# A selective-scan kernel: two states stacked on the partitions, all scan inputs turned on TensorE

## The reference

```python
xz = einsum('bld,ed->ble', x, W_in); xc, z = split(xz, 2)       # 256 inner channels each
xc = silu(causal_conv4(xc) + conv_b)
dbc = einsum('ble,re->blr', xc, W_x)                            # 8 for dt, 16 for B, 16 for C
dt = softplus(einsum('blr,er->ble', dbc[..., :8], W_dt) + b_dt)
A = -exp(A_log)                                                 # 256 x 16 states
def step(h, inp):                                               # over the 32 tokens
    h = exp(dt_t[:, :, None] * A) * h + (dt_t * x_t)[:, :, None] * B_t[:, None, :]
    return h, einsum('bdn,bn->bd', h, C_t)
y = (ys + xc * D_skip) * silu(z)
out = einsum('ble,de->bld', y, W_out)
```

## Time and profile before

| | us |
|---|---|
| three runs, median (lowest, highest) | 848.93 (847.19, 849.27) |
| span of the profiled execution | 847.5 |
| PE busy | 764.2 (90%) |
| DVE busy | 750.4 (89%) |
| ACT busy | 727.1 (86%) |
| POOL busy | 713.4 (84%) |

### The profile page before, as it was taken

How to read it: one execution, slowest core, us unless ns; L and a number is a source line. 1 busy time by engine, 2 the same in 40 slices (tenths; PEclk the granted TensorE clock), 3 DMA queues, 4 the chain that set the end, 5 groups by cost and what they waited for, 6 DMA issues and landing times.

```text
span 847.5 us, 13089 instructions
## 1 busy us (share of the span) xinstructions
PE 764.2 (90%) x4510; PEld 386.1 (46%) x4510; DVE 750.4 (89%) x476; ACT 727.1 (86%) x1301; POOL 713.4 (84%) x337
## 2 busy tenths in 40 slices
PE   8788989999999999898999998989999987678998
PEld 5534434343435453434353533434444433337876
DVE  2798999999999999999999999999999999984241
ACT  4889999999999999999999999999999999545050
POOL 0658999999999999999999999999999999980000
PEclk9799989999999999999999999999999999799999
DMA  7808071544335251527070717262534436000001
GB/s 201 299 4 272 26 250 52 184 143 158 144 113 189 84 210 57 229 67 260 29 271 28 251 51 251 76 223 79 195 108 145 159 101 224 2 1 1 1 37 63
DMA packets 39146, 110.97 MB, mean 131 GB/s; under 512 B 7244, under 2 KB 9384, under 8 KB 39080
## 3 DMA queue, kind: packets, MB, share of 16 engines
q1 hardware_dynamic: 37724, 109.84, 37.2%
q10 hardware_dynamic: 1356, 0.29, 0.2%
HBM read 106.97 MB, written 3.15 MB: 130 GB/s over the span
## 4 chain that ended last, share of the span: by engine, by line
DVE 27%; POOL 21%; PE 19%; issue 18%; ACT 12%; SPq 2%; DMA 1%; DVEq 0%; POOLq 0%; ACTq 0%
DVE state L894 13%; POOL state L598 10%; DVE bank L894 10%; POOL state L589 10%; PE bank L1283 8%; PE bank L1089 4%; ACT bank L694 3%; PE bank L1082 3%; ACT product L718 3%; ACT state L705 2%; DVE state L904 2%; POOL u L612 1%; ACT L753 1%; ACT dt L758 1%; SPq L406 1%
## 5 line engine op out<-in xcount | busy, mean ns | idle before, releaser
L598 POOL TENSOR_TENSOR state<-state,wide 128x1024 f32<-128x1024 f32 x161 | 378.1, 2368 | 10.0 <-DVE state L894 10.0
L589 POOL TENSOR_TENSOR state<-u,wide 128x1024 f32<-128x1024 f32 x128 | 301.7, 2369 | 11.9 <-PE bank L1089 11.7
L1089 PE MATMUL bank<-state,ident 64*64 64x512 f32 x2048 | 264.1, 627 | 0.5 <-POOL state L598 0.3
L894 DVE TENSOR_TENSOR_SCAN state<-state,bank 128x1024 f32<-128x1024 f32 x95 | 214.9, 2272 | 2.8 <-PE bank L1082 2.8
L718 ACT ACTIVATE product<-u_tok,b_tok 128x256 f32<-128x256 f32 x512 | 213.0, 499 | 2.3 <-PE bank L1082 1.8
L1082 PE MATMUL bank<-ident,product 128*128 128x128 f32 x1024 | 143.4, 285 | 67.9 <-ACT product L718 32.4
L1082 PEld LDWEIGHTS bank<-ident,product 128*128 128x128 f32 x1024 | 115.7, 146 | 164.2 <-issue 95.9
L694 ACT ACTIVATE bank<-dt,a_neg 128x512 f32<-128x512 f32 x256 | 166.0, 680 | 25.5 <-DVE state L894 16.8
L705 ACT ACTIVATE state<-dt,a_neg 128x512 f32<-128x512 f32 x256 | 167.0, 715 | 0.6 <-PE bank L1089 0.6
L894 DVE TENSOR_TENSOR_SCAN state<-bank,state 128x1024 f32<-128x1024 f32 x66 | 149.9, 2270 | 0.8 <-ACT bank L694 0.8
L894 DVE TENSOR_TENSOR_SCAN bank<-bank,state 128x1024 f32<-128x1024 f32 x62 | 141.6, 2284 | 3.8 <-ACT bank L694 2.9
(11 more groups left out here) (101 smaller groups left out, 509.3 us busy)
## 6 DMA issues: line engine op xcount, KB each, us to landing
wide<-bc_rows SPq DMA_DIRECT2D x176, 512.0 KB, 6.2
wide<-bc_rows SPq DMA_DIRECT2D x32, 256.0 KB, 3.5
x_t<-in_x_dram SPq DMA_DIRECT2D x4, 512.0 KB, 4.8
out_dram<-x_t SPq DMA_DIRECT2D x8, 256.0 KB, 2.0
k_room<-in_L_conv_w_dram SPq DMA_DIRECT2D x2, 576.0 KB, 4.7
bc_rows<-dbc SPq DMA_DIRECT2D x16, 64.0 KB, 1.6
state<-in_L_conv_W_in_dram SPq DMA_DIRECT2D x2, 256.0 KB, 3.9
x_tok<-in_x_dram ACTq DMA_DIRECT2D x1, 256.0 KB, 3.7
```

The costliest lines, as they stand in the source:

```text
L589: pool.tensor_tensor(tile(n), u[:, :, :], over_halves(b_wide[:, PLAIN.index(s), :]), ALU.mult).then_inc(plain_input, 1)
L598: pool.tensor_tensor(tile(n), tile(n), over_halves(c_wide[:, n % NST, :]), ALU.mult).then_inc(output_pool, 1)
L894: dve.tensor_tensor_scan(flat(target), flat(decay), flat(source), 0.0, ALU.mult, ALU.add).then_inc(scanned, 1)
L1089: return pe.matmul(y_sum[64 * h:64 * h + 64, b, :], weights[rows, :], source[rows, h, :], start=first, stop=last)
```

## The change

Two states now share a tile's partitions. A tile still has 128x1024, and an item still has 16 of them, but tile `2j + h` holds states `2j` and `2j + 1` (`STACK = 2`) of half of the channels: partition = 64 b + 32 i + c, with `i` the state of the pair. With this

- all inputs are turned: every state's product with B is made in token order, seven states' on ACT and nine states' on POOL (`POOL_B`, `products`), and PE turns all 16 tiles; every decay goes to SBUF and reads dt and A doubled to the stacked layout. dt is doubled by eight DMAs an item from SBUF to SBUF (`duplicate_dt`), A_log by eight loads;
- only C is broadcast, by four DMAs a pair of states to 32 partitions each (`spread_c`); B needs no broadcast;
- the sum over states is done by 64x32 blocks: the two tiles of a pair go to different columns, and each block adds two states (`sum_states`);
- POOL has eleven products with C and DVE five; `SLOTS` is 13 instead of 9; the order tables are new, and PE has 20 slots;
- the output is projected and added in quarters, 256 columns in each item from the fifth on, and all x groups are turned ahead of the first tile; the signs of the 3x3 weights are turned in one go in item 0 (`PE_KERNELS`, `ACT_KERNELS`), straight to the weights of the convolutions;
- ACT leaves out the table load between the gate and the softplus (`EXP_BETWEEN` is false), and the two rows of W_dt stand at different partitions (`DT_AT`).

The core of the diff:

```diff
-SLOTS = 9
+SLOTS = 13
-PRODUCTS = 3
+PRODUCTS = 2
-POOL_C = (0, 1, 2, 3, 7, 8, 10, 12, 14, 15)
+STACK = 2
+POOL_B = (2, 3, 4, 5, 6, 8, 10, 11, 14)
+ACT_B = tuple(e for e in range(NST) if e not in POOL_B)
+POOL_C = (0, 1, 2, 4, 5, 6, 8, 9, 10, 11, 14)
+PE_TAPS = {3: ((1, 4),), 4: ((1, 5), (1, 6), (1, 7)), 11: ((2, 0), (2, 1)), 12: ((2, 2),), 13: ((2, 3),)}
+PE_TURNS = {1: (0,), 2: (1,), 3: (2,), 4: (3,), 5: (4,), 6: (5,), 7: (6,), 8: (7,), 9: (8,), 10: (9,), 11: (10,),
+            12: (11,), 13: (12,), 15: (13,), 16: (14,), 17: (15,)}
+PE_SUMS = {0: (-4,), 1: (-3, -2), 2: (-1,), 8: (0,), 14: (1,), 15: (2,), 16: (3,)}
+POOL_PRODUCTS = {0: (5, 6), 1: (8,), 2: (10, 11), 4: (14,), 5: (18, 19, 20)}
+POOL_OUTPUTS = {0: (0,), 1: (1, 2, 3), 2: (4,), 3: (5, 6, 7, 8), 5: (9, 10, 11, 12, 13, 14, 15)}
+ACT_DECAYS = {0: (4, 5, 6, 7, 8), 3: (9, 10, 11, 12, 13), 5: (14,), 6: (15, 16), 7: (17, 18, 19)}
+ACT_PRODUCTS = {0: (7,), 1: (9,), 3: (12, 13), 4: (15,), 6: (16, 17)}
+ACT_KERNELS = (2, 2, 2)
+PE_KERNELS = 10
...
+            def duplicate_dt(k):
+
+                sp.wait_ge(dt_ready, HALVES * (k + 1))
+                wait(sp, decay_ready, HALVES * NST * (k - 1))
+                for b in range(2):
+                    for i in range(STACK):
+                        for q in range(2):
+                            first, source = 64 * b + CH32 * i, 64 * b + CH32 * q
+                            sp.dma_start(dt_dup[k % 2][first:first + CH32, q:q + 3:2, :],
+                                         dt[source:source + CH32, :, :]).then_inc(dup_loaded, 16)
...
             for k in range(ITEMS):
                 store_rows(k)
+                for j in range(STATE_PAIRS):
+                    if j == SP_DUP:
+                        duplicate_dt(k)
+                    spread_c(k, j)
...
-            def times_b(n):
+            def products(e):
+                wait(pool, u_tok_ready, 4 * k + 4)
+                wait(pool, b_tok_ready, k + 1)
+                wait(pool, turned_input, 2 * (e // STACK - PRODUCTS + 1))
+                for blk in range(BLOCKS):
+                    pool.tensor_scalar(state_product(e)[:, blk, :, :], by_pair(u_tok[:, blk, :]),
+                                       b_tok[k % 2][:, blk, i:i + 1], None, ALU.mult).then_inc(product_pool, 1)
...
+            def decays(n):
...
+                k, j, h = n // NST, n % NST // 2, n % 2
+                wait(act, dt_far, k + 1)
+                wait_slot_free(act, n)
+                for q in range(2):
+                    g = 2 * h + q
+                    act.activation(tile(n)[:, q, :], dt_dup[k % 2][:, g, :], ACT.Exp,
+                                   scale=a_st[k % 2][:, j, g:g + 1]).then_inc(decay_ready, 1)
...
-                    copy(u_tok[:, 2 * j:2 * j + 2, :].rearrange("p a d -> p (a d)"), work[1]).then_inc(u_tok_ready, 1)
+                    for b in range(2):
+                        copy(u_tok[:, 2 * j:2 * j + 2, :].rearrange("p a (g i c) -> p (a g) i c", i=2, c=CH32)[:, :, b, :],
+                             work[1].rearrange("p (g i q c) -> p g i q c", g=4, i=2, q=2)[:, :, b, :, :]).then_inc(u_tok_ready, 1)
...
             def scan(n):
...
+                wait(dve, turned_input, n + 1)
+                wait(dve, decay_ready, HALVES * (n + 1))
                 target = tile(n) if by_pool(n) else pair[n % PAIRS]
-                dve.tensor_tensor_scan(flat(target), flat(decay), flat(source), 0.0,
+                dve.tensor_tensor_scan(flat(target), flat(tile(n)), flat(pair[n % PAIRS]), 0.0,
...
             def turn_input(n):
...
+                i, h = n // 2, n % 2
+                if h == 0:
+                    wait(pe, product_act, products_of(ACT_B, i + 1))
+                    wait(pe, product_pool, products_of(POOL_B, i + 1))
                 wait_pair_free(pe, n)
                 for blk in range(BLOCKS):
-                    for h in range(HALVES):
-                        mm = pe.transpose(pair[n % PAIRS][:, h, 128 * blk:128 * blk + 128],
-                                          product[j % PRODUCTS][:, blk, 128 * h:128 * h + 128], ident[:, :])
+                    for q in range(2):
+                        g = 2 * h + q
+                        mm = pe.transpose(pair[n % PAIRS][:, q, 128 * blk:128 * blk + 128],
+                                          product[i % PRODUCTS][:, blk, 128 * g:128 * g + 128], ident[:, :])
...
-                wait_output(pe, n)
-                for b, h in QUARTERS:
-                    mm = sum_quarter(b, h, ident2[:, :], tile(n), False, n % NST == NST - 1)
+                for n in (2 * i, 2 * i + 1):
+                    wait_output(pe, n)
+                    for b, q in QUARTERS:
+                        g = 2 * (n % 2) + q
+                        rows = slice(64 * b, 64 * b + 64)
+                        mm = pe.matmul(y_sum[CH32 * g:CH32 * g + CH32, b, :], ident4[rows, :], tile(n)[rows, q, :],
+                                       start=False, stop=(j == STATE_PAIRS - 1))
+                    mm.then_inc(summed, 1)
```

More of the change, by code:

```diff
@@ L75 @@
+ACT_PRODUCTS = {0: (7,), 1: (9,), 3: (12, 13), 4: (15,), 6: (16, 17)}
+ACT_EARLY = {}
+PE_SLOTS = 20
+PE_Z = 5
 PE_DBC = 6
 PE_DT = 7
[L77 to L89, removed]
+PE_B_TOK = 10
+PE_U_TOK = (14, 15)
+ACT_XC = 0
+ACT_GATE = 1
+ACT_DBC = 2
+ACT_DT = 2
+ACT_B_TOK = 4
+ACT_U_TOK = (5, 6)
+POOL_U = 3
@@ L91 @@
+POOL_FAR = 4
+SP_DUP = 2
+EXP_BETWEEN = any(s in ACT_DECAYS for s in range(ACT_GATE + 1, ACT_DT + 1))
+LATE_SUMS = sum(e < 0 for pairs in PE_SUMS.values() for e in pairs)
+LATE_OUTPUTS = sum(e < 0 for tiles in POOL_OUTPUTS.values() for e in tiles)
+DVE_POST = 3
+DVE_OUT = 8
 POST_INSIDE = True
-AT_KERNELS = (8, 9, 10)
-LAST_POOL = tuple(s for s in DVE_C if 8 <= s <= 12)
+ACT_SIGNS = 1
+ACT_KERNELS = (2, 2, 2)
+PE_KERNELS = 10
+LAST_POOL = tuple(s for s in DVE_C if 8 <= s <= 11)
 AT_STATS = 8
@@ L360, in flat, with over_quarters, state_product, by_pair @@
             return halves.rearrange("p h n -> p (h n)")
-        def over_halves(row):
-            return row.unsqueeze(1).to_broadcast([128, HALVES, CHUNK])
+        def over_quarters(row):
+            return row.unsqueeze(1).to_broadcast([128, 2, CHUNK])
+        def state_product(e):
+            i, j = e // STACK, e % STACK
+            return product[i % PRODUCTS][:, :, :].rearrange("p a (g i c) -> p a g i c", i=STACK, c=CH32)[:, :, :, j, :]
+        def by_pair(blk_tokens):
+            return blk_tokens.rearrange("p (g c) -> p g c", c=CH32)
+        def products_of(states, pairs):
+            return BLOCKS * before(states, STACK * pairs)
         def res_half(n):
@@ L425, in small_groups @@
                      w_x[m][:, :, :].rearrange("p a e -> p (a e)")),
-                    ("small", m, [w_dt_raw[m][:, h, :] for h in range(HALVES)], 128, (BC, XROWS), w_dt[m][BC:, :])]
+                    ("small", m, [w_dt_raw[m][:, h, :] for h in range(HALVES)], 128, (0, XROWS), w_dt[m][:, :])]
         def out_group(m):
@@ L784, in _ @@
                     for e in ACT_DECAYS.get(s, ()):
-                        if NST * k + e > 0:
-                            plain_decays(NST * k + e)
-                    for e in ACT_TURNED.get(s, ()):
                         if NST * k + e >= 0:
-                            turned_decays(NST * k + e)
+                            decays(NST * k + e)
                     prepare(k + 1, s)
-                    if k == 0 and s < 3:
-                        setup_copy(act, copy, BY_ACT[s - 3], setup_act)
+                    if k == 0:
+                        kernels(s)
                     for e in ACT_PRODUCTS.get(s, ()):
```

472 lines of the change are left out of this document (217 added, 255 removed).

## The result

The changed kernel takes 1096.6 us (median of 4 runs, 1093.8 to 1099.3) against 848.9 us (847.2 to 849.3) in the same session: a ratio of 1.293, with a 95% interval of 1.291 to 1.295. The forecast was 837 us. The profiled span is 1097.4 us.

What follows compares the result with a forecast made beforehand. DVE's chain was taken to set the pace, with POOL full as well. Profiled span 847.5 + 3 (start and first item) - 15 (fourteen items) = 835.5, plus 1.4 to the median: 837 us; likeliest 830 to 846, wide range 825 to 882.

Steps and rivals of the forecast that it cites:

- POOL's t: Time of each of POOL's 36 small products an item, in 27.6 us plus 36 t: 0.36 to 0.38 us, bounds 0.2 and 0.59.
- Rival One: POOL becomes the bound at its 36 small products, deciding from t = 0.43; total 866 us at 0.5, 911 at 0.59; chance 0.22.
- Rival Two: PE's sums over states: the eight blocks don't run beside each other; PE 50.0 us an item, 928 us in all; chance 0.07.
- Rival Three: Passage through two PSUM pairs eats the gain: period stays at 44.6 us, total time 849 to 855 us; chance 0.14.
- Rival Four: The start costs nothing and DVE has no new stall: 829 us or less; chance 0.09.
- one step less: DVE makes five C products instead of six: 1.35 us less an item, period 43.22 us if the stalls stay.
- the 0.3 us of stall that I added: DVE's added wait an item, for turned tiles passing two PSUM pairs, raising the period to 43.5 us.
- ACT: 40.8 against 40.8: ACT's work an item: fewer products, one table load less, narrower copies; 40.8 us, nothing for writing in runs of 32 columns.
- I had 41.9: PE's work an item: 8.9 us more for transposes, 8.2 less for sums over states; 41.9 us.
- The bytes moved: Data moved by the loads and other DMAs: claimed to fall to under half.
- The first scan: Start of the kernel: more loads and the decay's waits put DVE's first scan at 41 us instead of 32.8.
- The first item: Item 0: 43.5 + 5 = 49 us instead of 54.2, with a DVE stall of some 5 us ahead of scan 9.

Runs made afterwards that it cites:

- the fastest version: Against the 853.9 us version: dt's duplication before the C loads, convolution weights' loads behind them, their magnitudes and signs in first items, tiles 12 and 13's decays later; 823.7 us.

## Why the prediction was wrong, step by step

**The failed step** is POOL's t: "I take 0.36 to 0.38, because the new instruction also reads one tensor". It is 0.902 us. 27.6 + 36 x 0.902 = 60.1 us, and the period is 60.54: the equation was right, and the one number in it that no row showed was out by a factor of 2.4. Both ends of its bound failed for a reason that the runs name. Below, I took POOL's selections as relatives because they too read one tensor; their 0.05 us for 64 columns is 0.8 ns a column, the product with a scalar has 2.5. (0.29 + 2 x 0.05 is 0.39 us, not 0.40; it changes nothing.) Above, I took a quarter of the two-tensor product, 0.59 us, as a ceiling. That takes it that a form with one tensor is not dearer per column than one with two, and that a quarter of the columns is a quarter of the time; here the columns of the scalar form cost 2.5 ns, against 1.68 with the column held still and at most 2.3 (2.32 us/1024) in the moving product that I quartered, and an instruction has 0.14 or 0.26 us of its own, by its form. The two-tensor product of 256 columns, at 0.572 us, would just have kept the bound.

The Trainium skill's figure for short bodies of one input (GPSIMD Engine Reference, section Elementwise — side-by-side cycle accounting, 1.03 cycles an element), which gave the estimate of 0.22 us, doesn't hold for this instruction, with its 2.5 ns a column; its 2.6 cycles an element for `tensor_tensor`, an estimate of 2.2 ns a column at 1.2 GHz, agrees with the 2.32 us for the 1024 columns of the product with C, but not with the 1.68 ns of the product whose second operand stands still.

**Rival One** was the mechanism, from its own deciding point (0.43) on; its price ended at 911 us because its t ended at 0.59.

**Rival Two** falls: the sums are 119.8/14 = 8.6 us an item against 16.4 in the earlier trace rows, so eight blocks run side by side as four did: 7.8 us less, where I took 8.2. **Rival Three** falls by the run with three quarters of POOL's C products left out, and by the fastest version, which leaves out nothing and has a period of 42.99 us. **Rival Four** falls: the start did cost.

**What held.** DVE: one step less gave 44.57 - 1.35 = 43.22 us; the run that relieves POOL has 42.96, without the 0.3 us of stall that I added. ACT: 40.8 against 40.8, and its products at 163.8/392 = 0.418 us lose nothing by the broken write. PE: I had 41.9; it is 550.40/14 = 39.3 where the granted clock is 0.99 of full speed, and 617.95/14 = 44.1 after, at 0.88. The bytes moved fell from 110.97 to 60.43 MB, not quite to half.

**What was mis-sized.** The first scan: 46.1 us after, not 41. I named three parts (A_log's issues, the magnitudes behind the weights, dt's duplication). The version that moves all three, and the second item's taps, has it at 36.8; no run splits their sum. A_log's eight issues and the x copy behind them:

```profile
3.98 5.11 ACTq L418 DMA_DIRECT2D gate<-in_L_conv_A_log_dram  x8
...
10.41 0.60 ACT L661 ACTIVATE x_t<-bank 128x512 f32<-128x512 f32 x1
```

The pieces cost 0.64 us each, not 0.25 to 0.49, and the copy came 4.3 us later than in the earlier trace rows. That cost more than the delay. PE stood idle for 4.01 us before its first taps, and ran them from 11.07 to 17.20 us at a mean granted clock of 0.59 of full speed, for the most part at the lower of its two levels (1.2 GHz). Eight records of the same kind took 3.60 us from 19.44 us on at 1.00, the upper level (2.4 GHz), and 3.61 at the start of the kernel before, where PE had no such idle time. These 2.6 us were in no term of mine.

```profile
11.07 6.16 PE L1073 MATMUL bank<-x_t,w_tap 128*128 128x512 f32 x8 [4.01 <-ACT x_t L661]
...
19.44 3.60 PE L1073 MATMUL bank<-x_t,w_tap 128*128 128x512 f32 x8
```

The first item, where POOL's C products are cut to a quarter, takes 53.1 us, not 49 (43.5 + 5 is 48.5): besides the 5.25 us ahead of scan 9, which I had, DVE waits there 5.6 us for turned tiles, which I hadn't. That run's 838.6 us stand close to my 837 by luck, because errors cancel: against my sum +6.0 (first scan at 47.0), +4.1 (first item), -7.6 (period), -1.3 (last item 51.3) and +0.1 behind it.

## What to carry to other kernels

Before work is moved to an engine in a form that its trace doesn't show, let the range reach as far as the form can go: a bound from another instruction held here neither for a smaller size nor for another kind of operand. On GpSimd a column held still as the second tensor, in one instruction over all blocks, did in 1.87 us what four products with a scalar did in 3.6; with that form, one state's product moved to ACT and the orders changed, the stacked kernel runs in 0.972 of the time of before. And where one engine has no rest, a part moved to it is multiplied by its count: 36 x 0.52 us more than I took is 18.8 us, sixteen times.

## What the runs showed of the hardware

- A GpSimd product of a tensor and a scalar per partition (fp32, 128 partitions, 256 and 512 columns): 0.26 us fixed and 2.5 ns a column; 0.09 us less for 256 columns if the scalar is a number. Eight runs of 32 columns cost as much to write as one of 256 (0.902 and 0.898 us).
- A GpSimd product of two tensors whose second operand stands still along the columns: 0.14 us fixed and 1.68 ns a column (0.572 us for 256, 1.865 for 1024). The product with C, with a moving one, took 2.32 us for 1024.
- DVE scanning or idle made no difference to the step of the product with a scalar (0.902 us beside both).
- TensorE: eight blocks of 64x32 run beside each other as four of 64x64 did: 119.8 us for 1786 records after against 229.6 for 1792 in the earlier trace rows.
- The mean granted clock of TensorE over the fourteen items, as a share of full speed, was 0.97 before, 0.88 after, where PE waited for POOL (busy for 617.95 of 847.50 us), and 1.00 in the fastest version (549.36 of 601.90). Behind 4.01 us of idle time at the start it was 0.59, and eight tap records took 6.16 us instead of 3.60.
